# Scaling GpSimd's share of the weight chunks on GpSimd instead of ScalarE, with four smaller moves at the start

## What is computed

```
# layer 0, for each sequence b
scale = cond @ norm_w.T + 1
h  = x * scale * rsqrt(mean(x*x) + 1e-6)
val, gate = split(h @ up_w.T)                 # 2 x 1024
h  = val * gelu(gate)
hq = round(h * 127/max|h|) * max|h|/127       # per position
wq = clip(round(down_w / m), -1, 1) * m       # m = mean|down_w|
x  = x + hq @ wq.T

# layer 1
Wd_b = Wd + 0.1 * (cond @ Wdd.T + bdd)        # 128 x 256 for each b
Wu_b = Wu + 0.1 * (cond @ Wdu.T + bdu)        # 256 x 128 for each b
out  = x + relu(x @ Wd_b.T + bd) @ Wu_b.T + bu
```

## Time and profile before

| what | us |
|---|---|
| three runs | 492.66, 492.7, 493.88 |
| the profiled execution, its own time | 491.39 |
| its span, first to last instruction | 489.6 |
| TensorE busy in it | 469.5 (96%) |
| VectorE busy | 387.7 (79%) |
| ScalarE busy | 364.7 (74%) |
| GpSimd busy | 265.4 (54%) |

### The profile page before, as it was taken

The page is one execution under the profiler, slowest core; times in us unless marked ns, Lnnn a source line. Parts: engine busy times, 40 slices in busy tenths (PEclk is TensorE's granted clock), DMA queues, the critical chain, the costliest instruction groups (busy, mean ns, idle before and its releaser), DMA issues.

```text
span 489.6 us, 9974 instructions
## 1 busy us (share of the span) xinstructions
PE 469.5 (96%) x3252; PEld 271.2 (55%) x3252; DVE 387.7 (79%) x778; ACT 364.7 (74%) x631; POOL 265.4 (54%) x680
## 2 busy tenths in 40 slices
PE   8969999999999999999999999999999999999955
PEld 8435555555555555555555555555555555555533
DVE  3798988998898887878778787877778777777683
ACT  4888999899896777777686768677777777667551
POOL 3277565675654557556565665665444444444452
PEclk9989999999999999999999999999999999999986
DMA  7958867587763575656645566664455544553443
GB/s 247 352 94 208 257 166 227 164 221 226 185 173 44 117 121 120 158 122 139 144 84 141 131 162 130 122 154 95 115 119 143 126 110 108 129 131 75 88 96 107
DMA packets 120547, 71.65 MB, mean 146 GB/s; under 512 B 104688, under 2 KB 105648, under 8 KB 118320
## 3 DMA queue, kind: packets, MB, share of 16 engines
q1 hardware_dynamic: 120336, 70.94, 58.6%
q10 hardware_dynamic: 160, 0.07, 0.1%
HBM read 37.44 MB, written 8.39 MB: 94 GB/s over the span
## 4 chain that ended last, share of the span: by engine, by line
PE 77%; DVE 6%; ACT 5%; issue 5%; POOL 3%; DMA 2%; SPq 1%; ACTq 0%; DVEq 0%; POOLq 0%
PE bank L825 57%; PE bank L835 10%; PE bank L873 4%; PE bank L863 4%; DVE xs_lo L621 2%; DMA xn_s<-in_xn 2%; PE bank L849 2%; ACT stage L441 2%; ACT wsplit L446 2%; DVE adapt L588 1%; ACT gel L471 1%; POOL wsplit L364 1%; DVE x L716 1%; ACT xs_hi L454 1%; POOL ad_lo L400 1%
## 5 line engine op out<-in xcount | busy, mean ns | idle before, releaser
L642 DVE SCALAR_TENSOR_TENSOR hid<-bank,rms,gel 128x512 f32<-128x512 f32 x128 | 95.8, 748 | 75.7 <-ACT gel L471 72.4
L825 PE MATMUL bank<-up_hi,xs_hi 128*128 128x512 f16 x512 | 153.1, 381 | 2.7 <-DVE hid L642 2.4
L825 PE MATMUL bank<-up_lo,xs_hi 128*128 128x512 f16 x512 | 152.8, 380 | 0.5 <-DVE up_lo L747 0.5
L471 ACT ACTIVATE gel<-bank,rms 128x512 f32<-128x512 f32 x128 | 87.6, 684 | 88.2 <-PE bank L825 87.1
L825 PE MATMUL bank<-up_hi,xs_lo 128*128 128x512 f16 x512 | 152.8, 380 | 0.0
L825 PEld LDWEIGHTS bank<-up_lo,xs_hi 128*128 128x128 f16 x512 | 50.1, 98 | 61.9 <-DVE up_lo L747 1.9
L825 PEld LDWEIGHTS bank<-up_hi,xs_lo 128*128 128x128 f16 x512 | 50.2, 98 | 60.7 <-issue 0.6
L650 DVE TENSOR_REDUCE amax<-hid 128x1 f32<-128x1024 f32 x63 | 76.9, 1220 | 2.2
L364 POOL TENSOR_TENSOR wsplit<-stage,wsplit 128x288 f16<-128x288 f32 x64 | 56.4, 911 | 38.5 <-ACT wsplit L446 38.5
L477 ACT ACTIVATE hid<-hid,amax 128x1024 f32<-128x1024 f32 x64 | 72.4, 1132 | 1.5 <-DVE amax L676 1.2
L835 PE MATMUL bank<-tern,qT 128*128 128x256 bf16 x512 | 67.2, 275 | 4.6 <-DMA qT<-qn 3.2
(11 more groups left out here) (89 smaller groups left out, 625.3 us busy)
## 6 DMA issues: line engine op xcount, KB each, us to landing
xT_s<-in_xT SPq DMA_DIRECT2D x32, 256.0 KB, 3.4
xn_s<-in_xn SPq DMA_DIRECT2D x32, 256.0 KB, 3.7
stage<-in_WddT SPq DMA_DIRECT2D x8, 1024.0 KB, 5.7
stage<-in_WduT SPq DMA_DIRECT2D x8, 1024.0 KB, 5.2
out<-out_s SPq DMA_DIRECT2D x31, 256.0 KB, 2.3
adapt<-in_up_wT SPq DMA_DIRECT2D x4, 512.0 KB, 7.5
x<-in_down_wT SPq DMA_DIRECT2D x1, 1024.0 KB, 11.5
qT<-qn SPq DMA_TRANSPOSE x64, 3.1
```

The source lines that it names most:

```text
L471: nc.scalar.activation(gel[:, c], u_gate[c][:], ACT.Gelu, scale=rms[:, t // TPB % XN_SLOTS, t % TPB:t % TPB + 1]).then_inc(gelu_done, 1)
L642: nc.vector.scalar_tensor_tensor(out=hid[:, t % 2, c * 512:(c + 1) * 512], in0=u_val[c][:], scalar=rms[:, t // TPB % XN_SLOTS, t % TPB:t % ...
L825: ins = nc.tensor.matmul(dst[:], a[:, t // TPB % 2, k, cols], w[:, c, k, v, :], start=(k == 0 and n == 0), stop=(k == KD - 1 and n == 2))
```

## The change

Five edits. GpSimd scales its 1152 columns in four pieces, in a new `scale_part` that stands in each step ahead of its `low_part`; ScalarE loses L441, and its L446 now waits for GpSimd. `base_sum` moves to GpSimd's step 2, and becomes three instructions. The three large instructions of `ternary` are spread: the first stays in step 1, the second stands at the head of step 2, ahead of `gate(2, 0)`, and the third behind it. TensorE runs 9 in place of 12 idle matmuls before the first `up`, and `up` takes its three passes in another order. SyncE loads sequence 2 ahead of chunk 1.

```
-IDLE_SECOND = 12
+IDLE_SECOND = 9
...
             sp.dma_start(bu_row[:], bu.to_broadcast([P, D])).then_inc(ld_small, 16)
+            load_x(2)
             load_chunk(1)
...
+            def scale_part(q):
+                pool.wait_ge(ld_stage[q % 2], slot_count(q, 2))
+                piece = POOL_COLS // POOL_PIECES
+                for i in range(POOL_PIECES):
+                    part = stage[:, q % 2, CHUNK - POOL_COLS + i * piece:CHUNK - POOL_COLS + (i + 1) * piece]
+                    ins = nc.gpsimd.tensor_scalar(part, part, W_SCALE, None, ALU.mult)
+                ins.then_inc(w_scaled, 1)
...
+            def base_sum():
+                pool.wait_ge(ld_small, 16 * N_SMALL)
+                nc.gpsimd.tensor_scalar(bias_raw[:], bias_raw[:], DELTA_SCALE, None, ALU.mult).then_inc(base_ready, 1)
+                pool.wait_ge(base_ready, 1)
+                nc.gpsimd.tensor_tensor(base[:], base[:], bias_raw[:], ALU.add).then_inc(base_ready, 1)
+                pool.wait_ge(base_ready, 2)
+                nc.gpsimd.tensor_scalar(base[:], base[:], A_SCALE, None, ALU.mult).then_inc(base_ready, 1)
...
                     dequantization(s - 2)
+                if s == 1:
+                    rsqrt(1)
+                for q in chunk(s, 0):
+                    scale_part(q)
                 for b in sequences(s, 0):
                     output_bias(b)
-                if s == 1:
-                    rsqrt(1)
+                if s == 2:
+                    base_sum()
                 for q in chunk(s, 0):
                     low_part(q)
...
-                nc.scalar.activation(stage[:, q % 2, first], stage[:, q % 2, first], ACT.Copy, scale=W_SCALE
-                                     ).then_inc(w_scaled, 1)
                 nc.scalar.activation(wsplit[:, q % 2, 0, rest], stage[:, q % 2, rest], ACT.Copy, scale=W_SCALE
                                      ).then_inc(w_hi_v, 1)
                 act.wait_ge(w_scaled, q + 1)
...
             for s in range(END):
+                if s == 2:
+                    ternary_second()
                 if s < NT:
                     gate(s, 0)
...
                     rsqrt_guess(1)
-                    ternary()
+                    ternary_first()
                 if s == 2:
-                    base_sum()
+                    ternary_third()
...
-                    passes = ((xs_hi, up_hi), (xs_hi, up_lo), (xs_lo, up_hi))
+                    passes = ((xs_hi, up_hi), (xs_lo, up_hi), (xs_hi, up_lo))
```

More of the change, by code:

```diff
@@ L340, in _ @@
                         store_last()
-                if s % TPB == 0 and s // TPB + 2 < B:
+                if s % TPB == 0 and 2 < s // TPB + 2 < B:
                     load_x(s // TPB + 2)
@@ L585, in evacuate @@
                 if q == 0:
-                    dve.wait_ge(base_ready, 2)
+                    dve.wait_ge(base_ready, 3)
                 dve.wait_ge(gen_full, 2 * q + n + 1)
@@ L593, in evacuate, with ternary_first @@
                     op0=ALU.mult, op1=ALU.add).then_inc(gen_done, 1)
[L595 to L602, removed]
+            def ternary_first():
                 dve.wait_ge(absum_full, 1)
@@ L610, in ternary, with ternary_second @@
                                         ).then_inc(tern_ready, 1)
+            def ternary_second():
                 dve.wait_ge(tern_ready, 3)
@@ L613, in ternary, with ternary_third @@
                                         ).then_inc(tern_ready, 1)
+            def ternary_third():
                 dve.wait_ge(tern_ready, 4)
@@ L821, in up @@
                             pe.wait_ge(up_hi_ready, c * KD + k + 1)
-                        if t == 0 and n == 1:
+                        if t == 0 and n == 2:
                             pe.wait_ge(up_ready, c * KD + k + 1)
```

## The result

The changed kernel takes 528.4 us (middle of four runs, 528.25 to 528.87) against 492.7 before: a ratio of 1.0725, 95% interval 1.0701 to 1.0749, 36 us slower. 509 was forecast, with 526 as the upper end. The direction and the place were right, the size was not: half of the loss was foreseen.

A forecast was written before the change was run, and what follows sets the result against it. TensorE bounds the kernel now; in the generator GpSimd's serial loop would take over. 6.5 us at the start plus six pairs at 1.8 (10.8) gave 17.3 on 491.4: 508.7, stated as 509 us, range 495 to 526.

The forecast's parts named there:

- What bounds the kernel, and where the change acts: TensorE, busy 15.08 of 15.65 us per generator pair; all gain or loss lies up to the generator's end.
- One serial loop on GpSimd: In the generator, scaling, ScalarE's L446 and low part follow in turn, adding two round trips of 1.28 us per pair.
- The price of a piece: Each GpSimd scaling of 128 x 288: 0.52 us, bounded by memset's 0.34 and the two-input instruction's 0.81.
- `base_sum`: GpSimd's step 2: two one-input instructions of 0.70 us each and a two-input one of 1.2, 2.6 us in all.
- The terms that were too dear: Low parts on GpSimd, taken from the earlier trace: 3.21 us in the even step, 3.62 in the odd.
- the 0.2 added for collisions: Per generator pair, GpSimd meeting VectorE's low part: half the difference of 3.62 and 3.21 us, bounds 0 and 1.1.
- The rule of exclusion: Two-SBUF-input VectorE and SBUF-reading GpSimd instructions exclude each other; pairs could lose 1.1 us, 5 us more in all.
- The Trainium skill's price: Estimate for GpSimd's scaling at 1.03 cycles an element: 0.25 us for 288 columns, 0.53 a piece with the fixed part.
- The start: GpSimd up to chunk 2's low part: it ends at 55.0 instead of 48.47, 6.5 us lost in full.
- It costs like the two-input instruction: Rival: GpSimd's scaling piece takes 0.81 us, 10.0 us lost at the start, pairs of 19.8; 526 us, chance 0.15.
- ScalarE's relief: Rival: without L441, gelu and `xs_hi` come 1.1 us earlier, saving 4.1 us in all; 487 us, chance 0.05.
- The clock behind TensorE's idle time: Some 8 us idle ahead of `generate(0)` lowers TensorE's clock; over 2 us spare per pair means no further cost.

## Why the forecast was right in kind and wrong in size

- *What bounds the kernel, and where the change acts.* Right. Only 1.1 of the 37.5 us come behind the generator, and the four other edits are worth nothing by themselves (1.0003).
- *One serial loop on GpSimd.* Right: two idle times per pair, 1.27 us each (1.28 forecast), both for L465. The run with two-column pieces shows that the loop costs next to nothing while it is shorter than TensorE's 15.1 us.
- *The price of a piece.* This step failed. "I take the fixed part from the tiny instructions [...] and the slope of memset: 0.28 + 286 x 0.83 ns = 0.52 us." It is 0.905 start to start: 0.2 us fixed and 2.5 ns a column. Memset's slope fits moving data (a copy takes 0.43 for 288 columns), not this arithmetic. The upper bound failed too: "the two-input instruction of the same shape" was taken as dearer than one with a single input, and it is cheaper (0.70 a piece in L365 where nothing stands beside it). The 0.81 of the earlier trace rows was itself stretched by VectorE. Twelve pieces at the start and 48 in six pairs, 0.385 each too cheap, are 23 us, more than the 19.4 that were missing; other terms were too dear.
- *`base_sum`.* 2.6 us forecast, 4.4 measured: the same error, two one-input instructions of 1.49 in place of 0.70.
- *The terms that were too dear.* The low parts were taken from the earlier trace rows, where VectorE's low part and input scaling stood beside them. In the changed kernel they meet less: 2.80 in place of 3.21 and 3.62. rsqrt was not too dear (3.33 forecast, 3.58 in the pair above). In that pair the scaling takes 3.4 us more than forecast, rsqrt 0.25 more and the low parts 1.3 less; the 0.2 added for collisions is inside the scaling's 3.95. That the sum missed by only 2.0 us a pair owes something to errors that cancel.
- *The rule of exclusion.* The row that the prediction puts beside it, L609, reads one tensor and one number per partition, so it is not of the kind that the rule names; VectorE's low part is. What it cost the scaling of a pair, 0.33 to 0.64 us, lay between the 0.2 and the 1.1 of the forecast.
- *The Trainium skill's price*, "GPSIMD Engine Reference", section 3.1, a port-bound body of up to two operations at 1.03 cycles an element, does not hold for this instruction: 2.5 ns a column are 3.0 cycles at that page's 1.2 GHz. The two-input price of 2.6 is near what is seen (by estimate, 0.80 us for the product of 288 columns, less the same 0.2 fixed, are 2.5 cycles). Here the measurements decide.
- *The start.* 6.5 us forecast at chunk 2, 12.2 measured. rsqrt(1) ended at 28.3 (29.3 forecast); the rest is scaling, `base_sum` and a collision of 0.9 us in the second chunk (4.51 in place of 3.62).
- *The rivals.* "It costs like the two-input instruction" (526 us) came nearest, in part by luck: its piece of 0.81 was too cheap and its low parts too dear, so that its pairs of 19.8 us met the measured 19.6. ScalarE's relief exists, 0.24 us a pair, and is only seen where GpSimd has time.
- *The clock behind TensorE's idle time.* TensorE waits for GpSimd in every pair of the changed kernel, so that there it can cost little, as forecast; no run tests it there. In the kernels where GpSimd does not bind the slow matmuls above are seen, but taking them away with 17 idle matmuls gave no more than 9 did.

## What to carry to other kernels

A free engine's busy share does not say that it can take work: lay its row end to end over one period, add the new work with every wait that it makes serial, and compare that with the period. Price an instruction from the same kind of instruction; where the trace has none, a move or a memset is no stand-in for arithmetic, and another kind of arithmetic was no upper bound here, so keep the range open upward. Durations taken beside a colliding engine already hold the collisions, and idle time that is filled can have been what kept two engines apart.

## What the runs showed of the hardware

- On GpSimd a multiplication of fp32 by a constant costs 0.2 us and 2.5 ns a column (215, 926 and 3124 ns for 2, 288 and 1152 columns), whatever the place and type of the result; a copy of 288 columns 0.43 us, a product of two tensors 0.80 us.
- VectorE's low part, which reads two tensors, and a GpSimd instruction that reads one or two hold each other up. A GpSimd piece that begins beside it loses what is left of it less 0.14 us, 0.33 to 0.93 us in these runs. VectorE's low part that begins beside a two-input piece of 288 columns took up to 1.72 us in place of 1.07, beside a one-input piece of 288 columns at most 1.13, beside the one-input instruction of 1152 columns up to 2.37. The section "Who interferes with whom" of the Trainium skill, "SBUF — State Buffer", has the exclusion; the trace agrees that one waits for the other, but they are not apart for a whole instruction: VectorE's low part ran its 1.07 us unstretched while the last 0.62 us of a one-input piece stood beside it.
- After 4.24 us of idle time the granted clock was 0.50, and TensorE's 512-column matmul pairs came every 0.85 us in place of 0.43, until some 5 us after the wait; with idle matmuls in 3.96 us of that gap the clock stayed at 1.00. The length of the idle time alone does not tell: after the same 2.44 us the clock was 0.51 in the kernel before (27.85 to 31.20) and 1.00 in the kernel with nothing but the scaling moved (27.75 to 30.30).
